# A decoder of four layers on one core: the impulse response of its state space kernel, as small GpSimd operations in the narrow cross attention

## The reference

```python
def _L2_xattn_ref(x, y, wq, bq, wk, bk, wv, bv, wo, bo):     # 16 heads of 8, context of 1444 rows of 96
    q = (x @ wq + bq).reshape(B, Sq, H, D).transpose(0, 2, 1, 3)
    k = (y @ wk + bk).reshape(B, -1, H, D).transpose(0, 2, 1, 3)
    v = (y @ wv + bv).reshape(B, -1, H, D).transpose(0, 2, 1, 3)
    ...
    attn = jax.nn.softmax(scores, axis=-1)
    ...

def _L2_ffn_ref(tgt, router_w, router_b, w1, b1, w2, b2, gamma, beta):
    ...
    rw = jnp.zeros_like(rw).at[..., 0].set(1.0)               # only the first expert counts
    h = jax.nn.relu(jnp.einsum('bsd,edf->besf', tgt, w1) + b1[None, :, None, :])
    ...

def s4d(x, log_dt, A_re, A_im, C_re, C_im, D_skip):           # in _L3_xattn_ref
    Bb, L, D = x.shape
    dt = jnp.exp(log_dt)
    A = A_re + 1j * A_im
    C = C_re + 1j * C_im
    dtA = dt[:, None] * A
    dC = C * (jnp.exp(dtA) - 1.0) / A
    powers = jnp.exp(dtA[:, :, None] * jnp.arange(L))
    K = 2.0 * jnp.einsum('dn,dnl->dl', dC, powers).real
    ...
    return y + x * D_skip                                     # y is by now x convolved with K
```

## Time and profile before

| What | Value |
|---|---|
| Time, median of 3 runs | 4985.25 us (4976.4 to 4988.59) |
| The profiled execution, its time | 5023.49 us |
| The profiled execution, its span (first to last instruction) | 5021.6 us |
| Busy: TensorE, its weight loads, VectorE, ScalarE, GpSimd | 85%, 60%, 57%, 39%, 31% of the span |
| Granted TensorE clock, mean over the span | 0.874 |
| cross_narrow in the trace | from about 2562 to 3468 us |
| ff2 in the trace | from about 3482 to 3570 us |
| ffg in the trace | from about 4680 to 4714 us |

### The profile page before, as it was taken

How to read it: one execution, slowest core, us unless ns; L and a number is a source line. 1 busy time by engine, 2 the same in 40 slices (tenths; PEclk the granted TensorE clock), 3 DMA queues, 4 the chain that set the end, 5 groups by cost and what they waited for, 6 DMA issues and landing times. The chain is left out here.

```text
span 5021.6 us, 88620 instructions
## 1 busy us (share of the span) xinstructions
PE 4259.1 (85%) x27918; PEld 2989.5 (60%) x27918; DVE 2843.6 (57%) x4430; ACT 1979.6 (39%) x3119; POOL 1539.6 (31%) x1111
## 2 busy tenths in 40 slices
PE   8899999999988988887869999998386666657699
PEld 4578888888866855734436555555153444444477
DVE  4345444454433444545645666664736999987433
ACT  2255555555542222223423545453133444440122
POOL 2265665665633312103410000000032333320043
PEclk8799999999988988888965999996687888778699
DMA  2000000000001201320012222220001111000021
GB/s 87 1 10 19 10 19 19 10 19 19 10 1 51 61 13 36 90 79 1 2 35 46 60 59 58 62 58 16 0 1 31 27 32 27 25 18 1 1 63 48
DMA packets 124781, 154.02 MB, mean 31 GB/s; under 512 B 86928, under 2 KB 110240, under 8 KB 124224
## 3 DMA queue, kind: packets, MB, share of 16 engines
q1 hardware_dynamic: 124352, 148.54, 11.7%
HBM read 110.25 MB, written 2.66 MB: 22 GB/s over the span
## 5 line engine op out<-in xcount | busy, mean ns | idle before, releaser
L1049 POOL TENSOR_TENSOR pexp_lo<-arena,pexp_hi 128x800 fp32r<-128x800 f32 x384 | 636.5, 1658 | 435.5 <-POOLq L1048 434.7
L2229 DVE TENSOR_REDUCE arena<-ps 100x1 f32<-100x482 f32 (+1 forms) x768 | 491.4, 658 | 288.3 <-DVEq L2216 278.7
L2109 DVE TENSOR_REDUCE arena<-ps 128x1 f32<-128x482 f32 (+3 forms) x624 | 393.1, 657 | 361.3 <-DVEq L2087 350.5
L1379 ACT ACTIVATE arena<-ps 128x800 f32<-128x800 f32 x384 | 322.1, 839 | 496.5 <-ACTq L1377 494.5
L3262 PE MATMUL ps<-kst,qs 96*100 96x482 f32 (+1 forms) x768 | 388.1, 507 | 41.2 <-PEq L3216 37.7
L1469 ACT ACTIVATE arena<-ps 128x800 f32<-128x800 f32 x384 | 315.6, 836 | 270.2 <-ACTq L1468 269.8
L995 POOL TENSOR_TENSOR max_diag<-w_const,arena 100x800 fp32r<-100x800 f32 x160 | 246.7, 1542 | 444.5 <-POOLq L993 444.5
L2531 DVE MATCH_REPLACE8 arena<-arena 128x1444 f32<-128x1444 f32 x208 | 348.4, 1719 | 0.0
L1380 ACT ACTIVATE pexp_hi<-ps 128x800 fp32r<-128x800 f32 x384 | 319.6, 832 | 0.0
L2633 DVE TENSOR_TENSOR arena<-ps,arena 128x400 f32<-128x400 f32 x256 | 147.1, 575 | 280.5 <-DVEq L2632 280.5
L1882 DVE TENSOR_REDUCE arena<-ps 100x8 f32<-100x800 f32 x160 | 158.3, 991 | 259.8 <-DVEq L1879 259.8
(11 more groups left out here) (396 smaller groups left out, 9507.9 us busy)
## 6 DMA issues: line engine op xcount, KB each, us to landing
ctxT<-in_ctxT SPq DMA_DIRECT2D x56, 541.5 KB
kst<-mid SPq DMA_DIRECT2D x128, 180.5 KB, 3.1
ctxk<-in_ctx SPq DMA_DIRECT2D x40, 528.0 KB
chunk<-in_ff_chunks SPq DMA_DIRECT2D x77, 193.0 KB, 2.4
arena<-gate_dram SPq DMA_DIRECT2D x64, 200.0 KB, 3.9
kst<-xn SPq DMA_DIRECT2D x64, 180.5 KB, 2.9
arena<-gate_dram SPq DMA_DIRECT2D x64, 100.0 KB, 2.6
arena<-in_ctxT SPq DMA_DIRECT2D x8, 541.5 KB
```

The source lines that it names most:

```text
L1049: own(nc.gpsimd.tensor_tensor(pexp_lo[p % 3][:, :, :], pexp[p % 3], pexp_hi[p % 3][:, :, :], ALU.subtract))
L1379: nc.scalar.activation(pexp[p % 3], of, ACT.Exp, scale=scale).then_inc(s.pexp_ready, 1)
L2109: peak = nc.vector.tensor_reduce(mparts[0:at.stop - at.start, m, c:c + 1], bank(k, z - a, at.stop - at.start), AX.X, ALU.max)
L2229: peak = nc.vector.tensor_reduce(mparts2[:, h, c:c + 1], bank(k, z - a, S), AX.X, ALU.max)
```

## The change

The impulse response leaves `feed_forward(2)` and goes to GpSimd, into `cross_narrow`. It is split into two generators, `impulse_angles` and `impulse_powers`; each `yield` ends a step of one to three operations. GpSimd's loop over the batch elements is written out, and after the three subtractions of an element it takes 15 steps: of `impulse_angles` for the elements 0 to 3, of `impulse_powers` from element 4 on. The three operations of 128x6400 and the reduction become, for each of ten groups of lags, two products and a subtraction of 128x640 and six halving additions. ScalarE's sine and exponential move into the batch element 3, between the second and the third exponential of the scores. The reciprocal of the magnitudes stays on VectorE, behind batch element 1. The working arrays move to the part of the arena that `cross_narrow` uses; the two products of 128x6400 are no longer kept.

```diff
+ROTATED_AT = 4
...
@@ the arena of cross_narrow
+    ssm = shared([128, 11, STATES])
+    inverse_a = shared([128, STATES])
+    powers = [[shared([128, LAGS + 1, STATES]) for part in range(2)] for base in range(2)]
+    scratch = [shared([128, LAGS * STATES]) for i in range(3)]
@@ GpSimd
+        def tt(o, a, b, op):
+            nc.gpsimd.tensor_tensor(o, a, b, op).then_inc(s.pool_done, 1)
+            pool.wait_ge(s.pool_done, 1)
+            pool.sem_inc(s.pool_done, -1)
...
+        def impulse_angles():
...
+            pool.wait_ge(loaded["tk"], 16)
+            tt(inverse_a, p["A_re"], p["A_re"], ALU.mult)
+            tt(row[8], p["A_im"], p["A_im"], ALU.mult)
+            yield
+            tt(inverse_a, inverse_a, row[8], ALU.add)
+            pool.sem_inc(s.magnitudes, 1)
+            yield
+            ts(z, p["log_dt"], 1 / 32, None, ALU.mult, ALU.bypass)
+            ts(dt, z, 1 / math.factorial(8), 1 / math.factorial(7), ALU.mult, ALU.add)
+            yield
+            for k in range(6, -1, -1):
+                ts(dt, dt, z, 1 / math.factorial(k), ALU.mult, ALU.add)
+                yield
+            for _ in range(5):
+                tt(dt, dt, dt, ALU.mult)
+                yield
...
+            pool.sem_inc(s.angles, 1)
+            ts(row[0], p["A_re"], dt, None, ALU.mult, ALU.bypass)
+            pool.sem_inc(s.decays, 1)
+
+        def impulse_powers():
...
+            pool.wait_ge(s.rotation, 2)
+            pool.sem_inc(s.rotation, -2)
...
+            pool.wait_ge(s.inverse_ready, 1)
+            pool.sem_inc(s.inverse_ready, -1)
...
+            def times(o, a, b, n):
+
+                t0, t1, t2 = (t.rearrange("p (r k) -> p r k", k=STATES)[:, 0:n, :] for t in scratch)
+                tt(t0, a[0], b[0], ALU.mult)
+                yield
...
+            for a in range(LAGS):
+                for part in range(2):
+                    tt(t[part], powers[1][part][:, a:a + 1, :].to_broadcast([128, LAGS, STATES]), powers[0][part][:, 0:LAGS, :], ALU.mult)
+                    yield
+                tt(t[0], t[0], t[1], ALU.subtract)
+                yield
+                half = STATES // 2
+                while half > 1:
+                    tt(t[0][:, :, 0:half], t[0][:, :, 0:half], t[0][:, :, half:2 * half], ALU.add)
+                    yield
+                    half //= 2
+                tt(kernel_l[:, LAGS * a:LAGS * a + LAGS].unsqueeze(2), t[0][:, :, 0:1], t[0][:, :, 1:2], ALU.add)
+                yield
...
-            with pool.Fori(0, B) as i:
+            angles, response = impulse_angles(), impulse_powers()
+            for b in range(B):
                 keys_low()
+                for part in range(15):
+                    next(angles if b < ROTATED_AT else response, None)
+            assert next(angles, True) and next(response, True)
@@ ScalarE, cross_narrow
+            def rotation():
+                act.wait_ge(s.angles, 1)
+                act.sem_inc(s.angles, -1)
+                nc.scalar.activation(ssm[:, 2:4, :], ssm[:, 2:4, :], ACT.Sin).then_inc(s.rotation, 1)
+                act.wait_ge(s.decays, 1)
+                act.sem_inc(s.decays, -1)
+                nc.scalar.activation(ssm[:, 0, :], ssm[:, 0, :], ACT.Exp).then_inc(s.rotation, 1)
+
+            def batch(par, first=False, more=True, rotate=False):
                 for p in range(4 * PAIRS):
+                    if rotate and p == 2:
+                        rotation()
...
-                batch(1)
+                batch(1, rotate=2 * i + 1 == ROTATED_AT - 1)
@@ ScalarE, feed_forward
-            if n == 2:
-
-                act.wait_ge(s.angles, 1)
...
@@ VectorE, cross_narrow
                 batch(2 * i + 1, 1)
+                if i == 0:
+                    dve.wait_ge(s.magnitudes, 1)
+                    dve.sem_inc(s.magnitudes, -1)
+                    nc.vector.reciprocal(inverse_a, inverse_a).then_inc(s.inverse_ready, 1)
                 batch(2 * i + 2, 0)
@@ VectorE
-        def impulse_response():
...
@@ VectorE, feed_forward
-            if n == 2:
-
-                dve.wait_ge(loaded["tk"], 16)
-                impulse_response()
             for g in range(NG):
```

More of the change, by code:

```diff
@@ L599, in build @@
     filled[0] = 0
[L600 to L606, removed]
     logits = shared([S, B, 16])
@@ L1079, in cross_heads, with ts @@
             batch(1, more=False)
+        def tt(o, a, b, op):
+            nc.gpsimd.tensor_tensor(o, a, b, op).then_inc(s.pool_done, 1)
+            pool.wait_ge(s.pool_done, 1)
+            pool.sem_inc(s.pool_done, -1)
+        def ts(o, a, c1, c2, op1, op2):
+            nc.gpsimd.tensor_scalar(o, a, c1, c2, op1, op2).then_inc(s.pool_done, 1)
+            pool.wait_ge(s.pool_done, 1)
+            pool.sem_inc(s.pool_done, -1)
+        def impulse_angles():
+            p = {k: W("tk", k) for k in ("A_re", "A_im", "log_dt")}
+            dt, z, row = col[:, 8:9], col[:, 9:10], [ssm[:, i, :] for i in range(11)]
+            pool.wait_ge(loaded["tk"], 16)
[14 more added lines that the diff above has]
+                yield
+            ts(row[1], p["A_im"], dt, None, ALU.mult, ALU.bypass)
+            yield
+            ts(row[4], row[1], 1 / (2 * math.pi), ROUND, ALU.mult, ALU.add)
+            ts(row[4], row[4], ROUND, None, ALU.subtract, ALU.bypass)
+            yield
+            part1 = 6.28125
+            part2 = float(np.float32(np.round((2 * math.pi - part1) * 2 ** 20) / 2 ** 20))
+            for part in (part1, part2, 2 * math.pi - part1 - part2):
+                ts(row[5], row[4], part, None, ALU.mult, ALU.bypass)
+                tt(row[1], row[1], row[5], ALU.subtract)
+                yield
+            ts(row[2], row[1], math.pi / 2, None, ALU.add, ALU.bypass)
+            ts(row[5], row[2], math.pi, 2 * math.pi, ALU.is_gt, ALU.mult)
+            yield
+            tt(row[2], row[2], row[5], ALU.subtract)
+            ts(row[2], row[2], 3.1415925, -3.1415925, ALU.min, ALU.max)
+            yield
+            ts(row[3], row[1], 3.1415925, -3.1415925, ALU.min, ALU.max)
+            pool.sem_inc(s.angles, 1)
+            ts(row[0], p["A_re"], dt, None, ALU.mult, ALU.bypass)
+            pool.sem_inc(s.decays, 1)
@@ L1456, in sums @@
                 act.sem_inc(s.o_kept, 1)
-            def batch(par, first=False, more=True):
+            def rotation():
[6 more added lines that the diff above has]
+            def batch(par, first=False, more=True, rotate=False):
                 for p in range(4 * PAIRS):
+                    if rotate and p == 2:
+                        rotation()
                     act.wait_ge(s.scoresT, 1)
```

178 lines of the change are left out of this document (75 added, 103 removed).

## The result

The kernel after takes 4969.53 us (median of 20 runs, 4914.19 to 5038.54), the kernel before 5003.37 us (20 runs beside them, 4968.53 to 5032.83). The ratio is 0.9921, interval 0.9894 to 0.9947: 26 to 53 us faster. The sign and the gain (46.6 us forecast, a ratio of 0.9906) fit both; the time itself does not: 4969.53 lies 4.5 us above the upper end of the range.

What follows compares the result with a forecast made beforehand. VectorE's impulse response was taken to bound the third feed forward. -53.6 (stage) - 2.6 (layernorm) + 3.1 (rotation) + 6.5 (clock) = -46.6 us, from the median 4985.25 to 4938.6 us; range about 4920 to 4965.

Steps and rivals of the forecast that it cites:

- the range: Whole kernel: about 4920 to 4965 us around the forecast time of 4938.6 us.
- What bounds the stage: Third feed forward (ff2): VectorE's impulse response chain sets its end; TensorE waits 51.00 us.
- The sign that the prediction set: ff2 takes 32 to 34 us to the next layernorm if the forecast is right.
- The twin's price: ff2 falls from 86.96 us to the 33.39 of ffg, the fourth feed forward: 53.6 us gained, up to 54.9.
- The layernorm's 2.6 us: Layernorm behind ff2: 18.22 us becomes 15.60 as behind ffg, 2.6 us gained.
- GpSimd's work at nothing: Narrow cross attention: about 128 us of operations and 31 of gaps on GpSimd, hidden by its waits, cost 0.
- the slots: GpSimd, narrow cross attention: the heaviest batch element's small operations take 17 us, with gaps 19.
- the cover of 43 us: Narrow cross attention: GpSimd waits about 43 us per batch element between key subtractions, hiding the added work.
- The `tensor_scalar` rival: GpSimd's first slot: nine operations at 5071 ns make it 10 us late, once; 4949 us, chance 0.04.
- The rotation: ScalarE, fourth batch element: sine and exponential delay TensorE 3.1 us and likely bring one clock fall, 6.5 us.
- The long low clock: Narrow cross attention: TensorE stays at 0.50 after the stall, 41 us lost; 4973 us, chance 0.12.
- Contention with VectorE: Narrow cross attention: GpSimd's operations hold up VectorE, TensorE loses 90 us; 5022 us, chance 0.06.

Runs made afterwards that it cites:

- the two edits of the kernel before: Kernel before without the four longest VectorE operations of the impulse response: ff2 27.6 us shorter; without ScalarE's sine, exponential and VectorE's wait for them: ff2 83.27 us.
- a second dose of it: Kernel after with every GpSimd product, sum and scaling of the impulse response done twice: median 4966.38 us, ratio to before 0.9937.
- e5_four_times: Kernel after with every GpSimd product, sum and scaling of the impulse response done four times: 5057.74 us.
- e6_two_inputs: Kernel after with four more 128x400 VectorE products, both inputs in SBUF, in each batch element of the narrow cross attention: 5158.60 us.
- a0_after: Kernel after, unchanged, in a second set of runs: median 4955.77 us, ratio to before 0.9901.
- e8_six_rotations: Kernel after without the impulse response, plus six rotations on unused data between second and third exponential of six batch elements: 4997.90 us, ratio 0.9985.
- e9_six_in_gap: As the six-rotation kernel, with the rotations moved behind the exponential of step 4, ahead of the next keys: 4925.73 us, ratio 0.9861.

## Why the prediction was right, and where it was off

**What bounds the stage**: right, and shown by the two edits of the kernel before. The sign that the prediction set, 32 to 34 us for ff2, was passed: it takes 29.4 to 31.1.

**The twin's price**, 53.6 us with 54.9 as its end: 56.2 us at 30.7, 57.5 in the first profile; mis-sized by 3 us. The forecast had to choose whether Relu behind the square root table loads a table, and chose the twin with its load of 1.28 us; no load is there. The Trainium skill (ScalarE: Activation LUTs, "Table sets: the hidden batching unit") had said that Relu is in every set, and the trace agrees. The other 1 to 2 us go with the clock, 0.84 to 0.88 in ff2 against 0.80 in the twin; no run separates it from Gelu and the rest of the twin. The layernorm's 2.6 us came as 2.4 to 2.6.

**GpSimd's work at nothing**: right by its own steps, the price of an operation to some 10 ns, the slots (19 us estimated, 16.9 measured behind the keys), the cover of 43 us. That it costs nothing holds at equal clock, to some 2 us; by the ratios up to 18 us for a second dose of it are not excluded. The `tensor_scalar` rival is gone: the prediction took the nine of the first slot for operations of 64 elements, they have one, and cost some 255 ns each.

**The rotation**, 3.1 us for the wait and 6.5 for one fall of the clock, 9.6 in all. In the first profile it was 3.6 us over two elements, in three others 16.6 to 26 (in e5_four_times a low stretch from 2744 to 2778 us came first, in e6_two_inputs the clock was low at the rotation), and over six rotations 10 to 12 us each in timed runs. That the mean was so well sized is partly luck: the 6.5 us were the mean of two falls that came by themselves, and those behind the rotation are of very unlike length. The reason given ("likely to bring one fall") was too weak, since every such wait at full clock brought a fall. The wait itself was 2.2 us, near the lower bound of 2 and not at the 3.1 that was taken.

**The rivals.** The long low clock at 41 us is what the forecast's 6.5 us shades into: in a0_after the clock stayed at 0.50 for most of the element behind the rotation, and the two elements cost 26 us more; no profile has one of 41 us behind the rotation. Contention with VectorE does not come about, and for the reason given: the same GpSimd operations do hold up products with two SBUF inputs.

**The sum** with measured terms is -56.2 - 2.5 + 10.3 = -48.4 us (10.3 is a sixth of the 62 us of the six rotations), the forecast -46.6; the two ratios give -39.5 and -49.6 us.

**The step that failed** is the last one: the 46.6 us were taken from a median of three runs, 4985.25 us. Twenty runs of the kernel before give 5003.37, so 18 of the 31 us by which the forecast time is too low are the base, not the change; the rest is the difference between 46.6 and the 33.8 us of the two medians (39.5 by the ratio). The profiled execution, 38 us above the three runs, was a sign that runs of this kernel spread over 60 us and more with the clock, and the range should have had that at both ends; it had 9 us at the lower end alone.

## What to carry to other kernels

Price a removed stage by a twin in the same trace, and moved work by a line through two shapes of the same engine, then ask of the receiving stage how long that engine really waits for data there: idle time summed over a stage is no cover by itself: VectorE's 30% here did not hide four short products an element. Look for the place where a short piece of work makes TensorE wait least: the same 3 us on ScalarE cost 10 to 12 us more at one place than three exponentials later. Where times follow the granted clock, compare kernels at equal clock, and don't take the base of a forecast from three runs.

## What the runs showed of the hardware

- A wait of 2.2 us on TensorE brought the granted clock down from 1.00, to a mean of 0.50 to 0.66 over the 10 us that followed, in all ten places where it met the full clock (five profiles with one rotation, five places in e8_six_rotations). Behind the eight rotations in the gap, with waits of 0.39 to 0.45 us, it stayed at 1.00 for that time; but falls without a rotation came behind waits of that size too, as in e9_six_in_gap at 3247 us. The low level then lasted from under 10 us (the kernel after) to over 50 us (a0_after), with TensorE busy 9.8 to 10 us in each 10: what ends it is not settled here.
- GpSimd's two-input operation costs 2.14 ns an element and 177 ns beside it from 64 to 640 elements (in the kernel after 315 ns at 64, 860 at 320, 1550 at 640); a copy of 640 elements 717 ns.
- A GpSimd operation and a VectorE product with two SBUF inputs delay each other, in both directions (e6_two_inputs: the product up to 1.21 us in place of 0.57, the GpSimd operation 1.87 in place of 1.55), while VectorE's reductions from PSUM stay at 0.66 us.
